# A graph attention kernel: 14 places in the ring of one-hots instead of 11, and two sums moved behind the counting

## The reference

```
def gat_layer(x, W, a_s, a_d, b, edge_index):
    h = (x @ W).reshape(n, H, C)
    alpha_s = einsum('nhc,hc->nh', h, a_s)        # one sum over 768 per node and head
    alpha_d = einsum('nhc,hc->nh', h, a_d)
    e = leaky_relu(alpha_s[src] + alpha_d[dst], 0.2)
    e = exp(e - segment_max(e, dst)[dst])
    alpha = e / (segment_sum(e, dst)[dst] + 1e-16)
    return segment_sum(h[src] * alpha[:, :, None], dst).reshape(n, H * C) + b

h = elu(gat_layer(x, W1, a_src1, a_dst1, b1))     # 8 heads
out = gat_layer(h, W2, a_src2, a_dst2, b2)        # 1 head
return layernorm(x + out)
```

## Time and profile before

| | us |
|---|---|
| median of 3 runs | 658.85 (658.73 to 663.57) |
| profiled execution, its own time | 660.23 |
| its span, first to last instruction | 658.4 |
| PE busy | 638.7 (97%) |
| DVE busy | 510.9 (78%) |
| ACT busy | 333.8 (51%) |
| counting on PE (L1094), first to last | 4.9 to 105.3 |

### The profile page before, as it was taken

How to read it: one execution, slowest core, us unless ns; L and a number is a source line. 1 busy time by engine, 2 the same in 40 slices (tenths; PEclk the granted TensorE clock), 3 DMA queues, 4 the chain that set the end, 5 groups by cost and what they waited for, 6 DMA issues and landing times.

```text
span 658.4 us, 9322 instructions
## 1 busy us (share of the span) xinstructions
PE 638.7 (97%) x3437; PEld 549.0 (83%) x3446; DVE 510.9 (78%) x927; ACT 333.8 (51%) x560; POOL 210.3 (32%) x121
## 2 busy tenths in 40 slices
PE   6999999999989999999999999999999999999995
PEld 4765567989878879988899889988998899878984
DVE  8899996798997977485956684677876787889466
ACT  7798972535614644353535444454436344524272
POOL 0000000132553550357124822473156514641130
PEclk9999999999999999999999999999999999999998
DMA  8413421115052520134112320325043403500002
GB/s 310 155 49 96 144 73 49 48 49 192 26 167 89 200 72 1 49 96 144 49 48 83 109 98 24 97 62 154 25 126 116 143 23 119 195 25 1 1 0 97
DMA packets 22173, 59.36 MB, mean 90 GB/s; under 512 B 2544, under 2 KB 2800, under 8 KB 22128
## 3 DMA queue, kind: packets, MB, share of 16 engines
q1 hardware_dynamic: 22128, 58.76, 27.5%
HBM read 54.03 MB, written 4.72 MB: 89 GB/s over the span
## 4 chain that ended last, share of the span: by engine, by line
PE 76%; DVE 19%; ACT 2%; issue 2%; DMA 0%; SPq 0%; DVEq 0%; ACTq 0%
PE O L1182 21%; PE R L1077 9%; PE R L1083 9%; PE R L1080 9%; PE R L1149 5%; PE R L1155 5%; PE R L1152 5%; PE O L1094 4%; DVE ohd L645 2%; DVE junk L681 2%; DVE hl L706 2%; DVE ohs L647 1%; DVE L L752 1%; DVE junk L808 1%; PE R L1099 1%
## 5 line engine op out<-in xcount | busy, mean ns | idle before, releaser
L1011 POOL TENSOR_TENSOR W2l<-Wr,W2h 128x768 fp32r<-128x768 f32 x48 | 98.9, 2067 | 212.6 <-ACT W2h L404 212.6
L1015 POOL TENSOR_TENSOR Pl<-L,Ph 128x512 fp32r<-128x512 f32 x34 | 53.8, 1594 | 174.3 <-ACT Ph L453 174.3
L1077 PE MATMUL R<-W1h,xTh 128*128 128x384 f32 x312 | 106.4, 341 | 0.0
L1080 PE MATMUL R<-W1l,xTh 128*128 128x384 f32 x312 | 105.4, 338 | 0.0
L1083 PE MATMUL R<-W1h,xTl 128*128 128x384 f32 x312 | 105.4, 338 | 0.0
L681 DVE CUSTOM_DVE_ANT_0 junk<-h,abc 128x768 bf16<-128x768 f32 x64 | 64.5, 1007 | 48.2 <-ACT h L416 46.8
L1182 PE MATMUL O<-W2h,gh 128*128 128x256 f32 (+1 forms) x384 | 79.9, 344 | 0.0
L1182 PE MATMUL O<-W2l,gh 128*128 128x256 f32 (+1 forms) x384 | 77.5, 337 | 0.0
L1182 PE MATMUL O<-W2h,gl 128*128 128x256 f32 (+1 forms) x384 | 77.2, 336 | 0.0
L416 ACT COPY h<-R 128x384 f32<-128x384 f32 x62 | 29.5, 478 | 82.3 <-PE R L1083 76.3
L1094 PE MATMUL O<-ohd,ohs 128*128 128x512 bf16 x255 | 61.9, 389 | 8.2 <-DVE ohs L647 5.7
(11 more groups left out here) (172 smaller groups left out, 1158.0 us busy)
## 6 DMA issues: line engine op xcount, KB each, us to landing
Wr<-in_W SPq DMA_DIRECT2D x101, 384.0 KB, 3.2
abc<-in_as SPq DMA_DIRECT2D x9, 384.0 KB, 4.5
abc<-in_ad SPq DMA_DIRECT2D x9, 384.0 KB, 5.9
h_rows<-h SPq DMA_DIRECT2D x8, 384.0 KB, 2.3
hl<-h_rows SPq DMA_DIRECT2D x8, 384.0 KB, 6.1
xin<-in_xT SPq DMA_DIRECT2D x6, 256.0 KB, 6.1
xr<-in_x SPq DMA_DIRECT2D x1, 1536.0 KB, 7.3
out<-res SPq DMA_DIRECT2D x4, 384.0 KB, 2.3
```

Source lines behind the costliest of these rows:

```text
L1011: e.tensor_tensor(W2l[:, m % N2, :], Wr[:, n, :], W2h[:, m % N2, :].bitcast(f32), ALU.subtract).then_inc(s_w2l, 1)
L1015: e.tensor_tensor(Pl[:, t, d0:d1], L[:, t, d0:d1], Ph[:, t, d0:d1].bitcast(f32), ALU.subtract).then_inc(s_Pl, 1)
L1077: e.matmul(bank[:, 0:HALF], xTh[:, f, xs], hi[:, ws], start=f == 0, stop=False)
L1080: e.matmul(bank[:, 0:HALF], xTh[:, f, xs], lo[:, ws], start=False, stop=False)
```

## The change

The ring has 14 places. The two pairs of sums of head 1 that stood before blocks 99 and 127 go behind the last one-hot: the first ahead of the last `accumulate`, the second behind it. The sums of head 0's tiles 2 and 3 stand before blocks 46 and 70 (43 and 67 before), and the first four accumulates before blocks 44, 76, 98 and 124 (41, 73, 95, 121). ACT's copies follow `OHR` by themselves, so they too come three blocks later.

```diff
-    OHR = 11
+    OHR = 14
...
-                if j in (24, 30, 43, 67):
-                    t = (24, 30, 43, 67).index(j)
+                if j in (24, 30, 46, 70):
+                    t = (24, 30, 46, 70).index(j)
                     if t == 0:
                         wait_abc(0)
                         e.wait_ge(s_xl, FT)
                     e.wait_ge(s_h32, 2 * t + 2)
                     sums_h(0, t, h32[:, t % 2, :], abc[:, 0, :, :])
                     low_h(0, t)
-                if j in (99, 127):
-                    t = (99, 127).index(j)
-                    if t == 0:
-                        wait_abc(1)
-                    e.wait_ge(s_h32, 8 + 2 * t + 2)
-                    sums_h(1, t, h32[:, t, :], abc[:, 1, :, :])
...
-                if j in (41, 73, 95, 121):
-                    accumulate((41, 73, 95, 121).index(j))
+                if j in (44, 76, 98, 124):
+                    accumulate((44, 76, 98, 124).index(j))
                 one_hot(j)
+            wait_abc(1)
+            e.wait_ge(s_h32, 10)
+            sums_h(1, 0, h32[:, 0, :], abc[:, 1, :, :])
             accumulate(len(GROUPS) - 1)
+            e.wait_ge(s_h32, 12)
+            sums_h(1, 1, h32[:, 1, :], abc[:, 1, :, :])
```

## The result

| | before | after |
|---|---|---|
| median of 10 runs, us | 658.88 | 655.33 |
| lowest and highest | 658.33, 663.57 | 654.57, 657.66 |
| profiled execution, its time and span | 660.23, 658.4 | 655.43, 653.6 |

The ratio of the runs that are compared is 0.9928, with a 95% interval from 0.9909 to 0.9948. The change is faster, by 0.5% by the medians and 0.7% by the ratio. Both lie inside 1%, yet the interval excludes no change. The medians differ by 3.55 us, where 3.56 were worked out. The ratio says 4.7 us, and so does the difference of the two spans (4.8); that is more than the change is worth. Four of the ten executions of before took 660.6 us or more, and one of the changed kernel took 657.66; without these five the medians are 658.71 and 655.33, 3.4 us apart.

A forecast was written before the change was run, and what follows sets the result against it. PE bounds the kernel, but in part of the counting DVE feeds it late. Losses of 0.93, 0.45 and 2.18 us, 3.56 together, all go: 658.85 - 3.56 = 655.3 us, from 654.6 to 656.2 (chance 0.82).

The forecast's parts named there:

- The sum: Whole program: 3.56 us off the median 658.85 gives 655.3; for the profiled execution, span 654.8 and time 656.7.
- A measurement of this kernel tells a change from none at about 1%, 6.6 us: Whole time: the gain counts as no change; chances faster 0.02, within 1% 0.96, slower 0.02.
- The bound and its size: Counting stage: DVE feeds PE late; PE loses 0.93, 0.45 and 2.18 us in three stretches, 3.56 together.
- The ring's 2.1 us: DVE from blocks 22 to 29: waits for free places shrink or vanish, putting DVE 2.1 us ahead.
- The sums' 1.86 us: DVE before block 99: moving one pair of head 1's sums away adds 1.86 us, a lead of 3.96.
- the margin: Block 99: DVE's lead of 3.96 us exceeds the 3.56 that PE needs by 0.4, the smallest margin.
- Cover in the new place: DVE behind its one-hots: moved pairs fit idle time before the last accumulate and the masks, costing nothing.
- The rest of the program: Behind the counting: every engine hangs on PE's last count, so no fixed point in time swallows the gain.
- Rival B: Behind the counting: some later stage ends by another clock and swallows the gain; time stays 658.9; chance 0.04.
- A: Counting: only moving the sums helps, since ACT becomes the late supplier; 1.7 us gained, time 657.2; chance 0.10.
- C: Counting: moved buffer addresses slow DVE's one-hots; a fifth slower gives 3.8 us more, 662.7; chance 0.02.
- D: Counting: PE could outrun its feed everywhere, so all of DVE's 5.8 us come through, 653.1; chance 0.02.

The follow-up runs named there:

- The ring alone: Kernel before with 14 ring places and later accumulates and head 0 sums, head 1's sums left before blocks 99 and 127; median 658.05 us, ratio 0.9986.
- the 83 later ones: Executions of the unchanged kernel before, measured beside the follow-up kernels; 39 took 660.68 us or more, the 44 others at most 660.2.

## Why the prediction was right, and where it was not

The sum and the mechanism held; the step that failed is the one from the sum to the chances, "A measurement of this kernel tells a change from none at about 1%, 6.6 us". It is taken up below.

**The bound and its size.** That PE loses 3.56 us by starving, read from the starts of half tiles, was right: the counting is 3.51 us shorter, and each of the three stretches came down to the undisturbed length. Had one summed the waits that the list shows, 2.7, the answer would have been 0.8 too small. Half tiles were predicted near 63.3, 72.5, 81.7 and 101.8 and stand at 63.25, 72.44, 81.63 and 101.73.

**The ring's 2.1 us.** Right in kind and size: the idle time at block 24 was given as 0.5, for ACT's copies, and is 0.42. The ring alone bought 1.99 us of counting; it has a lead of 2.1 and used 1.38 up to block 86, the rest at block 99.

**The sums' 1.86 us and the margin.** Alone they bought 1.46; together with the ring, all of the 2.18 at block 99. The margin was 0.49, for 0.4, but only where the program starts like the profile from which it was read: with a start 0.4 to 0.7 us earlier, 0.3 to 0.5 of the 3.56 are lost at block 99 again.

**Cover in the new place.** 3.4 and 1.3 us of idle time were predicted and 3.40 and 1.34 found. Another 3.0 us of sums ahead of the accumulate, beside the pair's 1.86, moved nothing.

**The rest of the program.** The shift came through: 546.7 at head 7, against 549.7 in the first profile of before, which had the short head 3, and 550.2 in the second. Rival B is out.

**The rivals.** A is refuted by the ring alone, C by DVE's one-hots, still 0.26 us apart (22.08, 22.61 and 22.86 for two `ohd`, an `ohs` and the next `ohd` in the profile after) and by DVE's busy time, 510.9 us before and after, D by the stretches of 9.19 and 10.91 us that did not shrink when PE stopped waiting.

**What was wrong: the step "a measurement of this kernel tells a change from none at about 1%".** I gave 0.96 to "within 1%" and 0.02 to "faster", and took a gain of 3.56 us as no more than could be told. The interval of the ratio is 0.2% to either side, so a gain of 0.5% stands clear of it, and this is a change that made the kernel faster. The text had the size right and then filed it under what can't be told. The range of the runs before, 658.73 to 663.57, had led me to 1%. Its upper part comes from executions with falls of the clock, by the 83 later ones: without such a fall they lie between 658.05 and 660.20. And an interval for medians of ten runs is narrower than the range of single runs.

**What was not foreseen.** The size by the ratio, 4.7 us. The sum against the profiled execution itself (span 654.8, time 656.7) was 1.2 too high, for the execution of before had a fall of the clock against it (1.7) and the half microsecond of head 3 in its favour, 1.7 - 0.5 = 1.2. I knew that this execution lay 1.4 above the median and did not ask why; the granted clock by stretches would have told. The prediction's second premise, a clock "granted in full in nearly every slice", rests on slices of 16.5 us, in which 3.4 us at half make a tenth at most. That the median was hit within 0.1 us is in part luck: it depends on how many executions have a fall, and starts alone differ by up to 2.1 us.

## What to carry to other kernels

When one engine feeds another through a ring, read the loss from the distance between equal landmarks of the fed engine, with and without waits, and not from the list of waits. The lead that a longer ring gives is bounded by the feeder's next wait for something else (here block 24's copies), and beyond that point places bought nothing here. Before moving work out of such a stage, find idle time on the same engine that is set by the engine it feeds: it moves along with the gain and stays as cover.

## What the runs showed of the hardware

- Rows of very small matmuls with no idle time of PE can be followed by a clock at half: behind 24 matmuls of 2 columns in 2.7 us the granted clock was 0.50 for 3.4 us, in about half of the executions (5 of 11 of the changed kernel lay 2.2 us or more above its fastest, with a mean clock of 0.995 or less), while in the first profile of the changed kernel no fall followed. With lots of 8 to 16 all 5 and all 12 executions kept a mean clock of 0.997 or more. The Trainium skill, "TensorE: Matmul & The Clock Gate", "HAM oscillation — how this bites in real kernels", tells of falls behind waits of PE; here PE had none.
- With a single wait of PE of 2.79 us went 3.4 us at 0.51, from 0.66 us before the wait's end on; together they cost 4.3 us (one profile).
- PE's first twelve counts took 4.91 us, and 3.38 when twelve transposes ran ahead of them.
- The clock's row says 1.00 in the first microseconds, though the first counts took 0.41 us each and later ones 0.215.
- Products of 48 x 3 matmuls ran at 335 or at 339 ns each in executions of the same kernel, before and changed alike, 0.48 us in sum.
